# Feed-forward weights quantised in place on interleaved blocks, with 16-bit bounds, in a decoder kernel

## The reference

```python
def _mx_quant(x, mbits):
    xb = x.reshape(s[:-1] + (s[-1] // BLOCK, BLOCK))
    amax = jnp.max(jnp.abs(xb), axis=-1, keepdims=True)
    shared_exp = jnp.floor(jnp.log2(jnp.where(amax > 0, amax, 1.0))) - EMAX   # EMAX = 2
    scale = jnp.exp2(shared_exp)
    return (_quant_elem(xb / scale, mbits) * scale).reshape(s)

gate = _mx_linear(x, w_gate)      # quant(x, 3 bits) @ quant(w, 1 bit).T
up = _mx_linear(x, w_up)
inter = jax.nn.silu(gate) * up
return _mx_linear(inter, w_down)
```

## Time and profile before

| | us |
|---|---|
| median of 3 runs (lowest, highest) | 1255.54 (1251.17, 1260.56) |
| the profiled execution | 1255.67 |
| its span, first to last instruction | 1253.8 |
| TensorE matmuls busy in the span | 1117.0 (89%) |
| VectorE busy | 897.8 (72%) |
| ScalarE busy | 609.8 (49%) |
| GpSimd busy | 520.1 (41%) |

### The profile page before, as it was taken

How to read it: one execution, slowest core, us unless ns; L and a number is a source line. 1 busy time by engine, 2 the same in 40 slices (tenths; PEclk the granted TensorE clock), 3 DMA queues, 4 the chain that set the end, 5 groups by cost and what they waited for, 6 DMA issues and landing times.

```text
span 1253.8 us, 17549 instructions
## 1 busy us (share of the span) xinstructions
PE 1117.0 (89%) x5813; PEld 888.1 (71%) x5818; DVE 897.8 (72%) x1480; ACT 609.8 (49%) x1193; POOL 520.1 (41%) x376
## 2 busy tenths in 40 slices
PE   4768843769999999999999999997999999987998
PEld 2333321338688888888888888775888989887887
DVE  6978998887686877777777778646657676755344
ACT  3533522322665656656565656552656565652111
POOL 1465220010564555555454646433465555550000
PEclk9878975879999999999999999998999999998999
DMA  8235515001102011010101000130202120111121
...
DMA packets 40900, 83.10 MB, mean 66 GB/s; under 512 B 10195, under 2 KB 18900, under 8 KB 37524
## 3 DMA queue, kind: packets, MB, share of 16 engines
...
...
## 4 chain that ended last, share of the span: by engine, by line
PE 76%; DVE 12%; ACT 4%; DMA 3%; POOL 2%; issue 2%; SPq 1%; ACTq 0%; DVEq 0%; POOLq 0%
PE PS L1584 20%; PE PS L1585 19%; PE PS L1586 19%; PE PS L1714 9%; PE PS L1450 1%; DVE blkamax L1069 1%; PE PS L1552 1%; PE PS L1775 1%; DVE arena L1099 1%; PE PS L1786 1%; DMA arena<-ek_dram 1%; DMA cs<-in_freqs 1%; PE PS L1569 1%; ACT arena L872 1%; DVE arena L1083 1%
## 5 line engine op out<-in xcount | busy, mean ns | idle before, releaser
L652 POOL TENSOR_TENSOR arena<-arena,rsum 128x768 f32<-128x768 f32 x192 | 283.3, 1476 | 387.1 <-DVE rsum L1256 387.1
L887 ACT ACTIVATE PTH<-PS 128x384 fp32r<-128x384 f32 x384 | 167.9, 490 | 247.1 <-PE PS L1714 246.8
L1251 DVE TENSOR_REDUCE nmax<-PS 128x1 f32<-128x768 f32 x192 | 182.9, 953 | 122.8 <-PE PS L1586 121.1
L1301 DVE TENSOR_TENSOR PTL<-PS,PTH 128x384 fp32r<-128x384 f32 x384 | 194.3, 547 | 8.0 <-ACT PTH L887 7.2
L872 ACT ACTIVATE arena<-PS,nmax 128x768 f32<-128x768 f32 x192 | 174.4, 908 | 29.2 <-DVE nmax L1251 28.7
L1714 PE MATMUL PS<-identf,arena 128*128 128x128 f32 x1152 | 158.7, 274 | 6.0 <-POOL arena L652 3.9
L1714 PEld LDWEIGHTS PS<-identf,arena 128*128 128x128 f32 x1152 | 129.7, 140 | 9.6 <-POOL arena L652 6.4
L1584 PE MATMUL PS<-PTH,VSH 128*128 128x512 f32 (+1 forms) x198 | 81.2, 410 | 2.4 <-DVE OTL L1272 2.0
L639 POOL TENSOR_TENSOR WQL<-arena,WQH 128x512 fp32r<-128x512 f32 x44 | 57.3, 1303 | 56.6 <-ACT WQH L712 56.6
L1584 PE MATMUL PS<-WOH,OTH 128*128 128x512 f32 (+1 forms) x180 | 74.9, 416 | 4.5 <-DVE OTL L1331 2.3
L1586 PE MATMUL PS<-PTH,VSL 128*128 128x512 f32 (+1 forms) x198 | 76.7, 387 | 0.0
...
## 6 DMA issues: line engine op xcount, KB each, us to landing
...
```

What stands on the lines that cost most here:

```text
L652: pool.tensor_tensor(PR[:, u % 4, :], PR[:, u % 4, :], rsum[:, u % 4:u % 4 + 1].broadcast_to([P, KEYS]), ALU.mult).then_inc(s["pn_ready"], 1)
L887: act.activation(fr(PTH[:, (u // 4) % 2, 3 * half:3 * half + 3, u % 4 * P:(u % 4 + 1) * P]), bank(B_PT[half])[:, 0:3 * P].rearrange("p (k ...
L1251: dve.tensor_reduce(nmax[:, slot:slot + 1], SC[pair][:, 0:KEYS], AX.X, ALU.max, negate=True)\
L1301: dve.tensor_tensor(fr(PTL[:, (u // 4) % 2, ks, cols]), bank(B_PT[half])[:, 0:3 * P].rearrange("p (k c) -> p k c", k=3), PTH[:, (u // 4) % ...
```

## The change

The weights come from the host in another order. Within each row, the columns are interleaved: instead of block after block (b, e), the order is element after element (e, b), so that element e of all blocks lie side by side, and the 32 elements of one block lie 16 elements apart (44 in the down weights). The rows of gate and up are interleaved in the same way, so that the inner activations come out in that order too.

The chunk is no longer divided by its scale. The exponent mask reads the upper 16 bits of each fp32 element and writes 16-bit values that are bf16 numbers, the powers of two of the elements (weight_exponents). Their maximum over a block is the block's power of two (weight_top). A quarter of it is the least step (weight_least), and the elements' powers are raised to it (weight_grid). The rounding multiplies this bf16 tile by a constant in the two scalar_tensor_tensor instructions (weight_shifted in place in the loaded chunk, weight_rounded to WQ8), and two more instructions cap the result at plus and minus 1.5 times the block's power of two (weight_capped), with the caps made by ScalarE from the small tile (caps). Bounds and steps are bf16 tables of 32 or 44 elements, read again for each of the 32 elements of the blocks. GpSimd has no part in the weights any more; its gathers follow one another. The chunks have four buffers instead of two; a buffer is loaded again once its chunk has been rounded. In VectorE's list the steps of chunk c and of chunk c + 1 alternate (weight_step).

act_quant has two forms: the normalised H is read in natural order and written in the interleaved one; the inner activations are read and written in the interleaved order.

The diff, without the declarations of names, the constants' counts, the removed lines of weight_normalised, weight_rounded, act_quant and scaled (shown above), and the calls whose arguments alone change:

```diff
@@ -198,17 +199,16 @@
-        WN2 = HT[:].rearrange("p k t -> p (k t)")[:, 0:IP]
         idle = EV0[:, 0, CTX // P:KK, :].rearrange("p k c -> p (k c)")
         blk2 = idle[:, 0:4 * (IP // MX)].rearrange("p (i b) -> p i b", i=4)
         parts = idle[:, 4 * (IP // MX):4 * (IP // MX) + RT * D // 8].rearrange("p (r b) -> p r b", r=RT)
-        blkinvs = (blkinv[:], blk2[:, 0], blk2[:, 1])
-        blkscales = (blkscale[:], blk2[:, 2], blk2[:, 3])
-        WX = at(49152, 2 * IP).rearrange("p (i n) -> p i n", i=2)
-        WN = at(60416, IP)
-        WM = at(66048, IP)
-        WN1 = at(129216, IP)
-        MAGIC_AT = ((129216 + 4 * IP, 129216 + 6 * IP), (77312, 77312 + 2 * IP))
+        def pair16(ap):
+            return [ap.bitcast(BF16)[:, i * (IP // MX):(i + 1) * (IP // MX)] for i in range(2)]
+        block_top, block_step = pair16(blkamax[:]), pair16(blkinv[:])
+        block_caps = list(zip(pair16(blk2[:, 0]), pair16(blk2[:, 1])))
+        WX = [at(offset, IP) for offset in (49152, 49152 + 4 * IP, 60416, 66048)]
+        grid_chunks = (at(129216, 2 * IP, BF16), HT[:].rearrange("p k t -> p (k t)")[:, 0:IP].bitcast(BF16))
         WQ8 = at(71680, 2 * IP, BF16).rearrange("p (i n) -> p i n", i=2)
         CTXT = at(77312, 2048).rearrange("p (k t) -> p k t", k=KT)
...
@@ -321,15 +321,29 @@
         KPAIRS = KV1 // 2
-        def weight_normal(c):
-            n = CHUNKS[c]
-            return (WN if c % 2 == 0 else WN1 if c < NCH else WN2)[:, 0:n]
+        def weight_chunk(c):
+            return WX[c % 4][:, 0:CHUNKS[c]]
+        def chunk_blocks(c):
+            return (2, D // MX) if c < NCH else (1, IP // MX)
+        def interleaved(ap, c):
+            t, _ = chunk_blocks(c)
+            return ap.rearrange("p (t e b) -> p t e b", t=t, e=MX)
+        def of_blocks(ap, c):
+            t, b = chunk_blocks(c)
+            return ap[:, 0:t * b].rearrange("p (t b) -> p t b", t=t)
+        def repeated(ap, c):
+            t, b = chunk_blocks(c)
+            return of_blocks(ap, c).unsqueeze(2).broadcast_to([P, t, MX, b])
         def weight_magic(c):
-            return at(MAGIC_AT[int(c >= NCH)][c % 2], CHUNKS[c], BF16)
+            return grid_chunks[int(c >= NCH)][:, c % 2 * IP:c % 2 * IP + CHUNKS[c]]
         def q_weights(G, j):
...
@@ -376,15 +390,15 @@
             sp.dma_start(dft_sb, dft).then_inc(s["dft_in"], 16)
             def load_chunk(c):
-                if c >= 2:
-                    sp.wait_ge(s["wx_used"], c - 1)
-                dst = WX[:, c % 2, 0:CHUNKS[c]]
+                if c >= 4:
+                    sp.wait_ge(s["wq_rounded"], c - 3)
+                dst = weight_chunk(c)
                 if c < NCH:
                     src = wgu[c * 2 * P:(c + 1) * 2 * P, :].rearrange("(t p) f -> p t f", p=P)
                     dst = dst.rearrange("p (t f) -> p t f", t=2)
                 else:
                     src = wd[(c - NCH) * P:(c - NCH + 1) * P, :]
-                sp.dma_start(dst, src).then_inc(s[f"wx_in{c % 2}"], 16)
+                sp.dma_start(dst, src).then_inc(s[f"wx_in{c % 4}"], 16)
             load_chunk(0)
             load_chunk(1)
...
@@ -611,27 +624,13 @@
                                         bass.IndirectOffsetOnAxis(ap=tapoff[:, r, k:k + 1], axis=0))\
                     .then_inc(tap_in[r], 16)
...
             pool.wait_ge(s["qs_ready"], 1)
...
+            for n in range(4):
+                context_quantised(n)
             pool.wait_ge(s["h2_out"], 32)
             pool.wait_ge(s["off_ready"], 1)
...
+            for n in range(RT * LAGS):
+                gather(n)
             def weight_lo(n, lo, raw, hi, heads=1):
...
@@ -747,13 +746,14 @@
                     act.activation(tap_diagonal(r, k), identf[:], ACT.Copy, scale=tapw[:, r, k:k + 1])\
                        .then_inc(s["dg_ready"], 1)
-            def magic(c):
-                act.wait_ge(s["wexp_ready"], c + 1)
+            def caps(c):
+                act.wait_ge(s["amax_ready"], c + 1)
                 if c >= 2:
-                    act.wait_ge(s["wq_rounded"], c - 1)
-                act.activation(weight_magic(c), WM[:, 0:CHUNKS[c]], ACT.Relu, bias=neg_magic[:, 0:1],
-                               scale=ROUND / 2).then_inc(s["magic_ready"], 1)
+                    act.wait_ge(s["wq8_ready"], c - 1)
+                for cap, sign in zip(block_caps[c % 2], (1.0, -1.0)):
+                    act.activation(of_blocks(cap, c), of_blocks(block_top[c % 2], c), ACT.Copy, scale=1.5 * sign)\
+                       .then_inc(s["caps_ready"], 1)
             squared(0)
             def context_clipped(n):
...
@@ -1062,50 +1062,104 @@
                         dve.tensor_tensor(fr(HTL[:, k, :]), HT[:, k, :], HTH[:, k, :], ALU.subtract)\
                            .then_inc(s["ht_lo"], 1)
...
+            def block_scale(src, nb, down):
+                step(dve.tensor_reduce(blkamax[:, 0:nb], src, AX.X, ALU.max, apply_absolute_value=True))
                 a = blkamax[:, 0:nb].bitcast(U32)
                 step(dve.tensor_scalar(a, a, EXPONENT, None, ALU.bitwise_and))
                 step(dve.tensor_scalar(blkscale[:, 0:nb], blkamax[:, 0:nb], TINY, down, ALU.max, ALU.mult))
                 step(dve.reciprocal(blkinv[:, 0:nb], blkscale[:, 0:nb]))
...
+            def weight_exponents(c):
+                dve.wait_ge(s[f"wx_in{c % 4}"], 16 * (c // 4 + 1))
+                halves = weight_chunk(c).bitcast(U16).rearrange("p (n h) -> p n h", h=2)
+                dve.tensor_scalar(weight_magic(c).bitcast(U16), halves[:, :, 1], EXPONENT16, None, ALU.bitwise_and)\
                    .then_inc(s["wexp_ready"], 1)
+            def weight_shifted(c):
+                w = weight_chunk(c)
+                dve.wait_ge(s["magic_ready"], c + 1)
+                dve.scalar_tensor_tensor(w, weight_magic(c), ROUND / 2, w, ALU.mult, ALU.subtract)\
+                   .then_inc(s["wx_shifted"], 1)
+            def weight_top(c):
+                dve.wait_ge(s["wexp_ready"], c + 1)
+                if c >= 2:
+                    dve.wait_ge(s["caps_ready"], 2 * (c - 1))
+                dve.tensor_reduce(of_blocks(block_top[c % 2], c),
+                                  interleaved(weight_magic(c), c).rearrange("p t e b -> p t b e"), AX.X, ALU.max)\
+                   .then_inc(s["amax_ready"], 1)
             def weight_rounded(c):
...
+                dve.wait_ge(s["wx_shifted"], c + 1)
                 if c >= 2:
                     dve.wait_ge(s["wt_psum"], c - 1 if c - 2 < NCH else NCH + 2 * (c - 2 - NCH) + 2)
...
+                dve.scalar_tensor_tensor(WQ8[:, c % 2, 0:CHUNKS[c]], weight_magic(c), ROUND / 2, weight_chunk(c),
+                                         ALU.mult, ALU.subtract).then_inc(s["wq_rounded"], 1)
+            def weight_least(c):
+                dve.wait_ge(s["amax_ready"], c + 1)
+                dve.tensor_scalar(of_blocks(block_step[c % 2], c), of_blocks(block_top[c % 2], c), 0.25, None, ALU.mult)\
+                   .then_inc(s["step_ready"], 1)
+            def weight_capped(c, which):
+                q = interleaved(WQ8[:, c % 2, 0:CHUNKS[c]], c)
+                if which == 0:
+                    dve.wait_ge(s["wq_rounded"], c + 1)
+                    dve.wait_ge(s["caps_ready"], 2 * (c + 1))
+                    dve.tensor_tensor(q, q, repeated(block_caps[c % 2][0], c), ALU.min).then_inc(s["wq_capped"], 1)
+                else:
+                    dve.wait_ge(s["wq_capped"], c + 1)
+                    dve.tensor_tensor(q, q, repeated(block_caps[c % 2][1], c), ALU.max).then_inc(s["wq8_ready"], 1)
+            def weight_grid(c):
+                m = interleaved(weight_magic(c), c)
+                dve.wait_ge(s["step_ready"], c + 1)
+                dve.tensor_tensor(m, m, repeated(block_step[c % 2], c), ALU.max).then_inc(s["magic_ready"], 1)
+            def weight_step(c):
+                ahead = c + 1 < len(CHUNKS)
+                if ahead:
+                    weight_exponents(c + 1)
+                weight_shifted(c)
+                if ahead:
+                    weight_top(c + 1)
+                weight_rounded(c)
+                if ahead:
+                    weight_least(c + 1)
+                weight_capped(c, 0)
+                if ahead:
+                    weight_grid(c + 1)
+                weight_capped(c, 1)
+            def act_quant(dst, src, n, q8, natural):
                 nb = n // MX
...
+                if natural:
+                    block_scale(blocks(src, n), nb, 16.0)
+                    step(dve.tensor_tensor(blocks(src, n), blocks(src, n), spread(blkinv, nb), ALU.mult))
+                else:
+                    block_scale(src.rearrange("p (e b) -> p b e", e=MX), nb, 16.0)
+                    src_eb = src.rearrange("p (e b) -> p e b", e=MX)
+                    step(dve.tensor_tensor(src_eb, src_eb, blkinv[:, 0:nb].unsqueeze(1).broadcast_to([P, MX, nb]),
+                                           ALU.mult))
```

(35 more changed lines are left out.)

66 lines of the change are left out of this document (12 added, 54 removed).

## The result

| | before | changed |
|---|---|---|
| median of 20 runs each, in turn, us | 1258.05 (1251.17 to 1261.82) | 1250.85 (1244.21 to 1253.96) |
| the profiled execution | 1255.67 | 1250.07 |
| its span | 1253.8 | 1248.2 |
| its mean granted TensorE clock | 0.944 | 0.944 |

The ratio is 0.9937, 95% interval 0.992 to 0.9954: the changed kernel is faster by 0.5 to 0.8%, about 8 us. I had forecast 1241, some 15 us less than the profiled time. The median of 1250.85 lies inside the range over all cases (1229 to 1265), just above the forecast's own range (1232 to 1249), and the change is under 1%: about half of the gain that I forecast.

What follows compares the result with a forecast made beforehand. VectorE's own instructions were taken to bound the weights' stretch. Its gain of 19.6 us, less 1.4 and 2.8 given back, made 15.4: 1255.7 to 1240, said as 1241; own range 1232 to 1249, all cases 1229 to 1265.

Steps and rivals of the forecast that it cites:

- What bounds: In the weights' stretch, 22.5 to 171.3 us, VectorE's own instructions set the end.
- Steps 1 to 3, 5 and 6: Weight chunks: scaling removed; advances in us per 1024 chunk: mask 0.61, two mixed roundings 1.15 each, three 16-bit operations 0.61 each, tiny multiplication 0.1.
- The rival that they run at one element per cycle: Weight chunks: the three 16-bit operations stay at 1.23 us, +22.6, giving 1264 us; chance 0.13.
- Step 4: Weights' block maximum over elements 32 or 88 bytes apart: 1.92 us for 1024 elements, 2.56 for 1408.
- The rival of 2.4 times the price per element: Stepped maxima and activation writes cost 2.4 cycles per element, together +16, giving 1257 us; chance 0.27.
- The waits: VectorE in the weights' stretch: wait for ScalarE's exponential (5.81 us before) gone, wait for chunk 8 4 us against 4.96.
- Step 7: Stretch 171.3 to 225: quantised activations written 32 bytes apart, four instructions on VectorE's path, 0.35 us more each: +1.4.
- Step 8: Feed-forward loop: maximum over 1408 elements stepping 176 bytes takes 2.56 us, 0.94 more, counted in blocks 0, 2, 3: +2.8.

Runs made afterwards that it cites:

- caps32: Changed kernel with the tables of steps and caps in fp32 instead of 16-bit, giving the three operations one 4-byte operand: 1272.93 us, ratio 1.0111.
- beside: Changed kernel with GpSimd multiplying its own scratch beside chunks 0 to 12, gathers spread between them: 1266.92 us, ratio 1.0077.
- contig: Changed kernel with the three stepped accesses made contiguous, for timing alone since its output differs: 1227.11 us, ratio 0.9772.
- tree: Changed kernel with the weights' block maximum taken by five element-wise maxima over halves instead of one stepping reduction: 1239.62 us, ratio 0.9848.
- read_side: Changed kernel with activations written in order and the step moved to the read of the 1-byte values: 1245.79 us, ratio 0.9904.
- probe: Changed kernel with 23 VectorE instructions added behind its last, timing stepped writes and reads; 512 2-byte writes 32 bytes apart took 2.30 us.

## Why the prediction came out as it did

**What bounds** held: VectorE's own chain. What was put on it (caps32, beside) or taken off (contig, tree, read_side) came back in the whole: in the traces the stretch ended 24.1 and 18.3 us later with caps32 and beside, and the runs took 22 and 16 longer; contig's rows give 23 and its runs 24. Only for tree do runs and trace differ by more (11.2 and 5.5 to 6.7).

**Steps 1 to 3, 5 and 6** held: 0.69 for the mask, 1.22 for the mixed operations, 0.69 and 0.89 for the 16-bit ones. The rival that they run at one element per cycle fell, and caps32 shows its price was rightly worked out.

**Step 4** held for 1024 elements (2.00 against 1.92; the whole chunk 6.71 against 6.68) and failed for 1408: 3.37 against 2.56, four times 0.8, 3.2 us. I had one rate for every step, and had not even kept to it: 1.92/1024 makes 2.64 of 1408 elements. The rival of 2.4 times the price per element was near for the 88-byte step (3.37, where it has 3.66) and wrong for the 32-byte one (2.00, where it has 2.7).

**The waits**: the exponential's was gone; chunk 8's was 2.65 against 4: VectorE wanted it at 88.2, as worked out, and it landed at 90.8, not at 92. The stretch took 131.1 against the forecast 129.2: the 3.2 us of step 4, less the 1.35 that the shorter wait gave back, a small piece of luck.

**Step 7 is the step that failed.** "By the ratio of step 4, (1.92 - 1.21)/1024 x 512 = 0.35 each: +1.4". That took the price of a read in GpSimd's rate for a write of 2-byte elements. It was 1.63 each, 6.5 us. The mechanism (a step on VectorE's path, all of it counted) was right, the size wrong by 4.7 times: 5.1 of the 7.5 us between the sum's 15.4 and the 7.9 of the ratio. In the probe 512 fp32 elements written 16 bytes apart take 1.07 us in all, the 2-byte ones 2.42; and the permutation as a read added 0.4 (read_side). The second term that was too small is step 4's for 1408 elements.

**Step 8** was nearly right: 2.73 against 2.56 each; the loop gave back 2.3, against 2.8.

Sum: 19.6 - 1.9 in the stretch, less 6.5 and less 2.3 in the loop, is 8.9 by the trace at the end of the loop (9.5 at the next block's first load), and (1 - 0.9937) x 1258 = 8 by the runs. The chances did not fit the range: I gave 0.11 to more than 1268, where the slower rival's own time was 1264 and the range ended at 1265. Step 7 had no bounds of its own: I took step 4's. Even the upper of these, 2.4 times 1.07 ns per element, makes 1.3 us of a write that took 2.33.
